# Making of counts in a graph network kernel: GpSimd makes three of sixteen cell tiles, and the copies of turned blocks are split anew

## The reference

```python
edge_index = jnp.stack([src, dst])
h = jnp.maximum(_layernorm(x, axis=-1), 0.0)
x = x + _L0_gnn_ref(h, edge_index, ...)   # attention, 4 heads
h = jnp.maximum(_layernorm(x, axis=-1), 0.0)
x = x + _L1_gnn_ref(h, edge_index, ...)   # two mean aggregations: segment_sum(x[src], dst)
h = jnp.maximum(_layernorm(x, axis=-1), 0.0)
x = x + _L2_gnn_ref(h, edge_index, edge_attr_2, ...)
h = jnp.maximum(_layernorm(x, axis=-1), 0.0)
x = x + _L3_gnn_ref(h, edge_index, edge_attr_3, ...)
```

## Time and profile before

| | us |
|---|---|
| median of 3 runs | 6663.62 |
| lowest and highest | 6661.44, 6674.17 |
| the profiled execution's own time | 6661.12 |
| its span in the profile | 6659.3 |
| stores of `adjacent`, first and last start | 1488.3, 1861.8 |
| mean granted clock of TensorE over the span | 0.917 of full |

### The profile page before, as it was taken

The page is one execution under the profiler, slowest core; times in us unless marked ns, Lnnn a source line. Parts: engine busy times, 40 slices in busy tenths (PEclk is TensorE's granted clock), DMA queues, the critical chain, the costliest instruction groups (busy, mean ns, idle before and its releaser), DMA issues. The chain is left out here.

```text
span 6659.3 us, 106073 instructions
## 1 busy us (share of the span) xinstructions
PE 4881.0 (73%) x34619; PEld 3665.0 (55%) x34619; DVE 4480.9 (67%) x11674; ACT 1826.4 (27%) x3144; POOL 4088.7 (61%) x4097
## 2 busy tenths in 40 slices
PE   5444444676638888888884667999999488888885
PEld 4444444455526666666662434555555366666664
DVE  7555555469957777777771315777776687877775
ACT  1222221458824444444440000000000133333332
POOL 1777777210047777777754254777775577767773
PEclk9999999989969989999996788999999799999997
DMA  4222221123332222222226582111111211111110
GB/s 73 79 78 78 78 78 55 24 57 158 160 85 57 56 56 56 55 55 56 56 47 208 201 262 70 38 37 37 37 37 32 28 21 19 20 19 20 19 20 13
DMA packets 389292, 438.88 MB, mean 66 GB/s; under 512 B 245539, under 2 KB 313104, under 8 KB 388765
## 3 DMA queue, kind: packets, MB, share of 16 engines
q1 hardware_dynamic: 202041, 289.96, 13.9%
q0 software_dynamic: 130592, 126.27, 11.2%
q10 hardware_dynamic: 56528, 21.19, 1.6%
HBM read 355.32 MB, written 82.34 MB: 66 GB/s over the span
## 5 line engine op out<-in xcount | busy, mean ns | idle before, releaser
L967 POOL DMA_INDIRECT at_far<-att_table,at_rec x1184 | 1198.7, 1012 | 759.1 <-DMA at_rec<-rec_r 398.6
L1680 POOL DMA_INDIRECT p_far<-table,p_rec x962 | 964.6, 1003 | 455.5 <-issue 284.9
L2487 PE MATMUL g_l_ps_sum<-g_l_row,g_l_of 128*128 128x392 f32 x3224 | 1063.4, 493 | 19.4 <-DVE g_l_of L2438 19.4
L2409 POOL DMA_INDIRECT g_l_got<-table,g_l_index x806 | 811.6, 1007 | 245.5 <-issue 228.1
L550 POOL DMA_INDIRECT rec_r<-so_r_rec,so_r_place x806 | 788.1, 978 | 245.5 <-issue 245.2
L2487 PEld LDWEIGHTS g_l_ps_sum<-g_l_row,g_l_of 128*128 128x128 f32 x3224 | 614.2, 191 | 469.2 <-DVE g_l_of L2438 20.5
L505 PE MATMUL so_r_look<-so_r_table,so_r_lo_t 128*128 128x26 f32 x1612 | 425.0, 434 | 313.1 <-DVE so_r_table L447 313.1
L2421 DVE TENSOR_SCALAR g_l_row<-g_l_iota,edge_row 128x784 f32<-128x784 f32 x806 | 500.6, 694 | 224.1 <-PE g_l_ps_sum L2487 223.9
L1398 DVE TENSOR_TENSOR p_spread<-at_far,p_mask 128x256 f32<-128x256 f32 x1184 | 444.3, 422 | 299.0 <-PE at_bank L1457 290.8
L1512 ACT COPY p_outer<-at_bank 125x512 f32<-125x512 f32 x1184 | 584.4, 779 | 62.8 <-PE at_bank L1457 62.8
L505 PEld LDWEIGHTS so_r_look<-so_r_table,so_r_lo_t 128*128 128x128 f32 x1612 | 417.5, 356 | 319.6 <-DVE so_r_table L447 165.0
(11 more groups left out here) (492 smaller groups left out, 6679.0 us busy)
## 6 DMA issues: line engine op xcount, KB each, us to landing
adjacent<-ad_by_chunk SPq DMA_DIRECT2D x74, 800.0 KB, 3.3
so_r_row<-pad_src SPq DMA_DIRECT2D x62, 832.0 KB, 6.1
g_l_counts<-adjacent SPq DMA_DIRECT2D x60, 800.0 KB, 7.0
g_l1d_counts<-adjacent SPq DMA_DIRECT2D x59, 800.0 KB, 7.2
so_r_low<-pad_lo_src SPq DMA_DIRECT2D x62, 416.0 KB, 4.5
at_far<-att_table,at_rec POOLq DMA_INDIRECT x1184
p_far<-table,p_rec POOLq DMA_INDIRECT x962
rec_r<-so_r_rec,so_r_place POOLq DMA_INDIRECT x806
```

Source lines behind the costliest of these rows:

```text
L967: pool.indirect_dma_start(out=far[b][:, t, :], out_offset=None, in_=g.att_table[:, :], in_offset=bass.IndirectOffsetOnAxis(ap=rec[b][:, t, ...
L1680: pool.indirect_dma_start(out=sl.far[b][:, t, :], out_offset=None, in_=table[:, :], in_offset=bass.IndirectOffsetOnAxis(ap=sl.rec[b][:, t, ...
L2409: pool.indirect_dma_start(out=got[b][:, j, :], out_offset=None, in_=table[:, :], in_offset=bass.IndirectOffsetOnAxis(ap=index[b][:, j:j + ...
L2487: last = nc.tensor.matmul(ps_sum[k][:], of4[b][:, j, :, :].rearrange("p k f -> p (k f)"), row1[b][:, j, k * COLS:(k + 1) * COLS], start=Fa ...
```

## The change

In `stage_adjacency`, DVE makes only the first 13 `cell1` tiles of a group; GpSimd makes the last three, by the same TENSOR_SCALAR, and counts them by `late_hots`, for which PE waits before its fourth set. GpSimd starts when DVE has made `cell` (`ready`), its program is written out for all 74 groups, and one of the 25 gathers follows the cells of each of the first 25 groups. The cut between the turned blocks moves from 16 to 11, so that DVE copies 11 blocks (128x1408) and ACT 14 (128x1792), and PE turns ACT's blocks first, before DVE's.

```diff
-    cut = 16
+    cut = 11
+    mine = GROUP - 3
...
+        ready, late_hots = sem("ready"), sem("late_hots")
...
-                collect_rows(pool, *collect, collected)
+                o_last, sums, to = collect[0].last, collect[1], collect[2]
+
+                def cells_of(n, b, first=False):
+                    if not first:
+                        pool.wait_ge(counted, (n - 2) * sets + sets)
+                    for j in range(mine, GROUP):
+                        last = nc.gpsimd.tensor_scalar(cell1[b][:, j, :], cells[:], cell[:, n * GROUP + j:n * GROUP + j + 1], None, ALU.is_equal)
+                    last.then_inc(late_hots, 1)
+
+                pool.wait_ge(ready, 1)
+                for n in range(groups):
+                    cells_of(n, n % 2, first=(n < 2))
+                    if n < NB:
+                        pool.indirect_dma_start(out=to[:, n, :], out_offset=None, in_=sums[:, :],
+                                                in_offset=bass.IndirectOffsetOnAxis(ap=o_last[:, n:n + 1], axis=0)).then_inc(collected, 16)
+                pool.wait_ge(collected, 16 * NB)
...
+                dve.sem_inc(ready, 1)
...
-                    for j in range(GROUP):
+                    for j in range(mine):
                         last = nc.vector.tensor_scalar(cell1[b][:, j, :], cells[:], cell[:, bass.ds(n * GROUP + j, 1)], None, ALU.is_equal)
...
-                    dve.wait_ge(turned, n * 2 + 1)
+                    dve.wait_ge(turned, n * 2 + 2)
...
+                        if k == mine // SET:
+                            pe.wait_ge(late_hots, n + 1)
...
-                    for h, (at, to, out) in enumerate(((0, cut, out_low), (cut, NB, out_high))):
-                        if h == 0:
+
+                    for h, at, to, out in ((1, cut, NB, out_high), (0, 0, cut, out_low)):
+                        if h == 1:
...
-                    act.wait_ge(turned, n * 2 + 2)
+                    act.wait_ge(turned, n * 2 + 1)
```

## The result

The changed kernel takes 6631.26 us, median of 5 runs (6621.36 to 6637.89), where the kernel before takes 6664.39 beside it. The ratio is 0.9944, with a 95% interval of 0.9933 to 0.9955: 37 us faster, between 30 and 45. The prediction was 6639, 24 us faster, in a range from 6617 to 6698. The profiled execution has a span of 6629.3 us, 30.0 less than before.

What follows compares the result with a forecast made beforehand. DVE was taken to bound the stage at 5.117 us a group; its own 4.29 plus 0.50 for GpSimd's comparisons gave 4.79, and 73 steps of -0.327 made -24 us: 6639, range 6617 to 6698.

Steps and rivals of the forecast that it cites:

- The stage's bound and place: Adjacency stage: DVE busy 70.00 of 70 us sets 5.117 us a group; any gain falls on the kernel's path.
- DVE's own work: DVE per group: copy 0.80, `lo1` 1.14 and 13 cell tiles at 0.181, together 4.29 us.
- ACT's work: ACT per group: four set copies at 0.738 and a long copy of 1.56, 4.51 us; period 4.57 with a small wait.
- The small wait between the last set copy and the long one: ACT before its long copy: some 0.05 us of waiting for its 14 turned blocks, ready at 2.99, ACT free at 2.95.
- GpSimd's cost to DVE: Three GpSimd comparisons beside DVE's cell tiles: 0.289 to 0.58 us each, taking 0.50 us a group from DVE.
- L: What one GpSimd operation takes from DVE: 0.166 us assumed, lower bound 0; forecast case 0.09 to 0.22, chance 0.32.
- the slow rival: GpSimd's comparisons slow DVE's cell tiles and what follows: at 0.43 us each, period 5.58, +34 us, 6698; chance 0.20.
- P: The group's period in the adjacency stage: 4.29 + 0.50 = 4.79 us, against 5.117 before.
- My own sign of being wrong: On GpSimd: the prediction is wrong if a comparison takes far more than an IOTA of its width, 0.289 us.
- The unblocked one: Rival: GpSimd blocks nothing on DVE (L below 0.09), ACT sets the pace at 4.57 us a group, 6623; chance 0.28.
- The moved gathers and the wait for `late_hots`: GpSimd and PE: both cost nothing; 2.1 us a group with a gather, free unless three operations take over 4 us.
- The order of the turned blocks: PE's turns: in the old order ACT would wait for all 25 blocks, until 3.68 us, and pay 0.7 us.

Runs made afterwards that it cites:

- e1_cut_only: The change with DVE making all 16 cell tiles and GpSimd none, keeping the new split and order: ratio 0.9968 against the kernel before, pace 4.818 us a group.
- e2: The change with the cut back at 16 blocks and the old order of turned blocks: ratio 0.9971 against the kernel before, pace 5.088 us a group.
- e4: The kernel before plus three GpSimd comparisons a group into an unread tile, started when a group's products end: ratio 1.0052, pace 5.689 us a group.
- e6: The kernel before plus three unread GpSimd comparisons a group, started only with DVE's copy out of PSUM: ratio 1.0027, pace 5.495 us a group.
- e7: The change with GpSimd also waiting until DVE made its 13 cell tiles of the group before: ratio 0.9936 against the kernel before, pace 4.692.
- e10: The change with four cell tiles on GpSimd in place of three: ratio 0.9958 against the kernel before, pace 4.827 us a group.
- e3: The change with the old order, PE turning DVE's 11 blocks before ACT's 14: ratio 1.0088 against the kernel before, pace 6.714 us a group.
- e5_change: The changed kernel, unedited, on a chip of the experiments: ratio 0.9953 against the kernel before, pace 4.653 us a group.
- e12: The kernel before plus three GpSimd MEMSETs a group into spare tiles, in place of comparisons: ratio 0.9993, pace 5.168 us a group.
- e11: The change with the cut at 10, one more block on ACT and one less on DVE: ratio 0.9954 against the kernel before, pace 4.771.

## Why the prediction was right, point by point

**The stage's bound and place.** Right. The gain is 33.7 us by the pace of the stores and 37 (30 to 45) by the runs. One thing is loose in the sum: 4.79 is made of starts in the middle of the stage, as the 5.17 of the earlier trace rows is, and was set against 5.117, the average that the last short steps lower. The same steps come at the end of the changed stage, so this moves the forecast by 4 us at most.

**DVE's own work.** Right to the hundredth: the copy 0.81 for a forecast 0.80, `lo1` 1.13, and with no GpSimd work the pace 4.818, or 4.84 from copy to copy, for 4.83 (`e1_cut_only`).

**ACT's work.** 4.63 to 4.64 for a forecast 4.57. The small wait between the last set copy and the long one, which I had put at 0.05, is 0.13: the long copy starts 3.08 to 3.09 behind the first set copy, not 2.95. By 0.062 a block ACT's blocks are there 0.09 before it starts (turns from 1601.73, copy at 1602.80), so it seems not to be a wait for PE, though no run separates it. (The 1651 ns in the sum should read 1649; the copy took 1652.)

**GpSimd's cost to DVE**, the term that no row showed, is where the sum was mis-sized, in both factors. The step said that a comparison lasts between 0.289 and 0.58 and that L is 0.166, so 0.50 a group. It lasts 0.78, outside my bounds; it takes 0.19 from DVE when it lies beside cell tiles (e2, e4), close to my L; and only two of three do, so the sum is 0.36 to 0.41, as one falls beside the copy out of PSUM, which e6 shows to be free. I had named that cover only as a point against the slow rival. With 0.36, P is 4.65 in place of 4.79 and the gain 34 in place of 24.

My own sign of being wrong came on, a comparison that takes far more than an IOTA: 0.78 to 0.289. The time stayed near the forecast all the same, because the price does not go with the length of GpSimd's instruction. My reason for L, that DVE is blocked for a part of the instruction and the rest is covered, has the right form: single tiles last 0.17 longer. But about two tiles are lengthened for each comparison, and part of that is not paid; that 0.166 and 0.19 lie so close is in part luck.

**The rivals.** The unblocked one (6623) is as near to the 6631 measured as the forecast (6639) is, so the time doesn't choose between them. ACT does come to its ceiling, but the rival's condition, L below 0.09, is false: tiles beside GpSimd are longer (e2, e4). I gave one mark for it, "ACT is busy for over 98%"; it holds (69.38 of 70) and was a poor one, since two engines can be full at once. The rival's own time was off too: with ACT's ceiling of 4.63 in place of 4.57 even a GpSimd that takes nothing would have gained only 0.05 a group more. The slow rival, GpSimd holding DVE for its whole instruction, is refuted by e2 and e4: 2.4 us of GpSimd cost 0.58.

The rule of the Trainium skill that I had weighed is in "SBUF — State Buffer", section "Who interferes with whom": a DVE instruction in a two-port mode, or one with two SBUF inputs beside a GpSimd instruction that reads, shares a lock with GpSimd, and whoever comes second fully blocks for the whole instruction. With GpSimd as the second it agrees: the comparison that starts inside `lo1`, which has two SBUF inputs, waits for its end (e7, 1.76 us in place of 0.78). Whether the cell tiles run in a two-port mode no trace shows. If they do, then with GpSimd first the rule says too much here: beside a comparison of 0.78 single tiles last 0.17 longer (e4). And in e6 `lo1`, to which the rule applies in any case, starts 0.14 behind a comparison (2004.78) and takes 0.15 more, not the rest of it. What the section says of a DVE instruction with at most one SBUF input outside the two-port modes, that it does not contend, agrees with the copy out of PSUM in e6 (1.13 as before).

**The moved gathers and the wait for `late_hots`.** Both free, as said, on the chip of the result, but with little to spare where I had seen much: with a gather GpSimd has 2.67 + 0.17 + 1.47 us of work in a group of 4.63, not the 2.1 of the sum, and waits only 0.27 to 0.34. On the other chips the spread gathers go with a gain. With four tiles GpSimd and its gathers become the slowest (e10, 5.14), and in the late start the groups with a gather take 4.9 on average; the bound that I had put at over 4 us of comparisons is near at their real length.

**The order of the turned blocks.** Right that it matters. At the full clock it is worth about 0.6 (5.24 in e3's first groups against 4.67 and 4.70), near the 0.7 of the sum; in the running stage it is 2.06, since the granted clock falls during the turns.

## What to carry to other kernels

Ask what work given to GpSimd costs a saturated VectorE beside it. Here each comparison beside VectorE's SBUF-to-SBUF tiles cost 0.19 us, about the 0.18 us tile that it saved, and only the one beside VectorE's copy out of PSUM was a gain. Price the move by where it falls in the other engine's cycle, not by its own duration. Before an order is changed so that TensorE waits, check the granted clock at which its fast figures were taken.

## What the runs showed that was not expected

A bf16 `is_equal` of 128x200 takes 0.78 us on GpSimd and 0.181 on VectorE from start to start, a factor of 4.3.

On the three chips of the experiments, 25 gathers issued in a row at the start of the stage go with late instructions on ACT. In e1, which has them in a row, ACT's rows below have idle times of 4.12, 6.19 and 3.42 us that no work of another engine in the trace explains:

```profile
1768.41 0.82 ACT L2138 CAST ad_counts<-ad_ps_set 128x800 bf16<-128x800 f32 x1 [4.12 <-issue]
...
1775.43 0.82 ACT L2138 CAST ad_counts<-ad_ps_set 128x800 bf16<-128x800 f32 x1 [6.19 <-remote]
...
1779.68 1.55 ACT L2138 CAST ad_counts<-ad_ps_set 128x800 bf16<-128x800 f32 x2 [3.42 <-remote]
```

From GpSimd's IOTA at the stage's start to the first store it is 41.0 us in e1 (1742.01 to 1783.0) and 26.7 in `e5_change` (1745.67 to 1772.4). The others fall in the same two classes: 39.2 to 39.3 with the gathers in a row (e4, e6, e12), 26.6 to 28.3 with the gathers spread (e2, e3, e7 to e11). These 12 to 14 us are about what the spread kernels gain on those chips beyond their pace: -34 - 13 = -47 for the change, if the kernel before behaves as e4, e6 and e12 do, and -44 was measured. On the chip of the result the gap did not show: 27.1 for the kernel before, with the gathers in a row, and 26.7 for the change. That the gathers cause it is inferred from this split of the twelve runs; no run moved the gathers alone, and the kernel before has no trace on those chips.
